# A macaron block on one core: V's second arrangement copied by VectorE ahead of its addition of the joined heads, not by two transfers

## What is computed

```
x = x + 0.5 * ffn(layernorm(x))
x = x + mla(layernorm(x))
x = x + 0.5 * ffn(layernorm(x))
```

```
h = shift_token(x)
q, k, v = split(h @ wqkv)                    # 8 heads of 64
q = l2norm(q) * qs;  k = l2norm(k) * ksc
q, k = rotary_xpos(q, k)
o = local_attention(q, k, v)                 # windows of 64 tokens, each looks at itself and the one before
x = x + o @ wo
h = layernorm(shift_token(x)) * lg + lb
a, g = split(h @ w1 + b1)
x = x + (a * gelu(g)) @ w2 + b2
```

## Time and profile before

| | before |
|---|---|
| median of 3 runs | 2024.47 us (2022.63 to 2025.84) |
| profiled execution | 2021.37 us, its span 2019.6 us |
| TensorE matmul busy | 84% |
| VectorE busy | 66% |
| ScalarE busy | 45% |
| GpSimd busy | 40% |
| the four engines in the turn from 257 to 303 us: TensorE, VectorE, ScalarE, GpSimd | 39.3, 35.1, 22.3, 24.2 us of 46.0 |

### The profile page before, as it was taken

How to read it: one execution, slowest core, us unless ns; L and a number is a source line. 1 busy time by engine, 2 the same in 40 slices (tenths; PEclk the granted TensorE clock), 3 DMA queues, 4 the chain that set the end, 5 groups by cost and what they waited for, 6 DMA issues and landing times. The chain is left out here.

```text
span 2019.6 us, 47886 instructions
## 1 busy us (share of the span) xinstructions
PE 1697.2 (84%) x19752; PEld 990.3 (49%) x19818; DVE 1336.6 (66%) x2021; ACT 916.4 (45%) x1455; POOL 799.7 (40%) x561
## 2 busy tenths in 40 slices
PE   3678888888889887799999994778888998988886
PEld 2345555555455554455555552445555555555543
DVE  4567776677766664577777764567777666667752
ACT  2234444454455443155555552344544554445442
POOL 3445445555554451100000002455555544555530
PEclk9789999999999999789999997889999999999998
DMA  4344454544444452322222200444344445554441
GB/s 144 40 77 67 75 76 75 86 72 69 75 73 75 77 78 54 98 74 83 80 75 92 92 22 7 67 73 86 69 67 73 77 68 82 77 92 80 76 84 32
DMA packets 82762, 148.55 MB, mean 74 GB/s; under 512 B 15039, under 2 KB 25715, under 8 KB 80371
## 3 DMA queue, kind: packets, MB, share of 16 engines
q1 hardware_dynamic: 81771, 142.81, 38.0%
q10 hardware_dynamic: 776, 2.68, 0.3%
HBM read 66.00 MB, written 16.52 MB: 41 GB/s over the span
## 5 line engine op out<-in xcount | busy, mean ns | idle before, releaser
L958 POOL TENSOR_TENSOR QK<-QK,RB 128x1024 f32<-128x1024 f32 x128 | 302.9, 2367 | 441.6 <-DMA RB<-RN 441.0
L798 DVE SCALAR_TENSOR_TENSOR TP<-banks,cols,tab 128x1024 f32<-128x1024 f32 x256 | 321.1, 1276 | 113.4 <-PE banks L462 88.8
L952 POOL TENSOR_TENSOR QK<-TP 128x512 f32<-128x512 f32 x128 | 164.8, 1287 | 252.1 <-DVE TP L798 193.6
L1295 ACT ACTIVATE PTL<-banks 128x1024 f32<-128x1024 f32 (+1 forms) x192 | 168.5, 885 | 168.5 <-PE banks L1202 168.5
L1370 DVE TENSOR_REDUCE NM<-banks 128x2 f32<-128x1024 f32 (+3 forms) x256 | 203.4, 821 | 57.2 <-PE banks L1171 56.1
L654 ACT ACTIVATE SQ<-banks 128x512 f32<-128x512 f32 x128 | 76.6, 599 | 290.0 <-PE banks L462 290.0
L821 DVE TRANSPOSE_TENSOR_REDUCE MX<-banks 128x16 f32<-128x512 f32 x256 | 160.3, 683 | 55.0 <-PE banks L499 55.0
L839 DVE TENSOR_TENSOR OT<-banks,OT 128x512 f32<-128x512 f32 x128 | 85.4, 688 | 151.8 <-DMA OT<-sums_d 138.3
L462 PE MATMUL banks<-HTH,wqkv_h 128*128 128x512 f32 x256 | 124.8, 487 | 68.4 <-POOL HTL L944 41.9
L953 POOL TENSOR_TENSOR QK<-TP 128x512 f32<-128x512 f32 x128 | 165.4, 1292 | 0.0
L532 PEld LDWEIGHTS banks<-PT,V 128*64 128x64 f32 x4096 | 128.5, 138 | 72.9 <-issue 47.5
(11 more groups left out here) (181 smaller groups left out, 3372.6 us busy)
## 6 DMA issues: line engine op xcount, KB each, us to landing
RB<-RN SPq DMA_DIRECT2D x512, 64.0 KB, 4.0
OT<-sums_d SPq DMA_DIRECT2D x128, 256.0 KB, 4.0
V<-V SPq DMA_DIRECT2D x32, 512.0 KB, 6.0
V<-V SPq DMA_DIRECT2D x32, 384.0 KB, 7.1
RB<-vars_d SPq DMA_DIRECT2D x32, 256.0 KB, 3.3
rows_d<-HIGH SPq DMA_DIRECT2D x32, 256.0 KB, 3.0
QS<-rows_d SPq DMA_DIRECT2D x32, 256.0 KB, 2.8
KS<-rows_d SPq DMA_DIRECT2D x32, 256.0 KB, 3.1
```

The source lines that it names most:

```text
L798: nc.vector.scalar_tensor_tensor(out=TP[:, o:o + 2, :], in0=BK[4 + z][:, :].unsqueeze(1).to_broadcast([P, 2, T]), scalar=q, in1=tab[:, e, ...
L952: nc.gpsimd.tensor_tensor(QK[:, m, 0, :], TP[:, 2, :], TP[:, 1, :], ALU.subtract)
L958: nc.gpsimd.tensor_tensor(QK[:, m, :, :], QK[:, m, :, :], RB[:, m, :].unsqueeze(1).to_broadcast([P, 2, T]), ALU.mult).then_inc(S["nr_ok"], 1)
L1295: nc.scalar.activation(PTL[:, G % 2, h0:h0 + 2, f * T:f * T + WIDTH_T[f]], PAIR[at_t(m) % RING][:, :, 0:WIDTH_T[f]], ACT.Exp).then_inc(S[" ...
```

## The change

The two transfers that fill V1 go, with SP's task `values`. VectorE gets a task `copy_values(u)` with the same two copies as `tensor_copy`: 64 partitions x 2048 and 64 partitions x 1536 elements of fp32. It waits for ScalarE's fourth slice of the unit (ve_ok) and, from the second unit on, for the attention that read the V1 of the unit before (pv_in). It stands in VectorE's list behind `statistics` and ahead of `residual`. The semaphore v1_ok now counts 1 a unit and not 32, and `attend` waits accordingly.

```
-                        def values(u):
-                            sp.wait_ge(S["ve_ok"], 4 * (u + 1))
-                            sp.dma_start(V1[0:W, :, :], V0[0:W, :, :]).then_inc(S["v1_ok"], 16)
-                            sp.dma_start(V1[W:P, 1:NT, :], V0[W:P, 0:NT - 1, :]).then_inc(S["v1_ok"], 16)
-
...
-                            run(values, n - 1)
...
-                            pe.wait_ge(S["v1_ok"], 32 * (u + 1))
+                            pe.wait_ge(S["v1_ok"], u + 1)
...
+                        def copy_values(u):
+                            dve.wait_ge(S["ve_ok"], 4 * (u + 1))
+                            if u >= 1:
+                                dve.wait_ge(S["pv_in"], 4 * u)
+                            nc.vector.tensor_copy(V1[0:W, :, :], V0[0:W, :, :])
+                            nc.vector.tensor_copy(V1[W:P, 1:NT, :], V0[W:P, 0:NT - 1, :]).then_inc(S["v1_ok"], 1)
+
...
                             run(statistics, n + 2)
+                            run(copy_values, n)
                             run(residual, n - 1, 7)
```

## The result

The changed kernel takes 2076.21 us (median of 4 runs, 2074.74 to 2077.93) against 2024.82 us before. Its ratio is 1.0245, 95% interval 1.0202 to 1.0288. The prediction on record was 2077.6 us. Its profiled execution took 2076.58 us, its span 2074.8 us.

A forecast was written before the change was run, and what follows sets the result against it. A chain through several engines, with GpSimd's L958, L944, L958 ahead of the scores, bounds each turn. 18 x 1.79 + 10 x 2.09 = 53.1 us on 2021.4 gives 2074.5, carried to the median 2077.6 us; range 2030 to 2104.

The forecast's parts named there:

- The chain: Feed-forward turn of about 45 us: a microsecond lost on GpSimd between 257.6 and 263.5 is lost for the whole turn.
- The removal at nothing: V1's two transfers per turn land some 17 us before `attend` reads them, so removing them is worth zero.
- The copies' duration: The two VectorE copies ahead of `residual` take 1.18 and 0.91 us, together 2.09 us.
- The one COPY in the earlier trace: SBUF to SBUF fp32 COPY of 512 elements, 365 ns, taken as half the PSUM slope to estimate the copies.
- the full-slope end: Upper estimate of the copies at the PSUM slope of 1.07 ns an element: 2.33 and 1.79, together 4.12 us.
- Hidden by VectorE's own queue at either slope: The copies fit VectorE's gap before `rotate` at 262.93; even 4.12 us end at 261.5 and `residual` at 262.9.
- The port: Copies block GpSimd's L958, L944, L958 on SBUF: +1.79 us in 18 turns, +2.09 in 10, 53.1 us; chance 0.59.
- Its sign: In the trace after, the second L958 starts about 5.7 us behind the last V slice instead of 3.9.
- rows 8: Trace rows of L318 beside L952/L953 and L969 beside L832, read as VectorE and GpSimd each waiting for the other's whole instruction.
- Half absorbed: Rival: VectorE's 1.27 us idle ahead of the maxima takes part of each 1.9 us; 18 us, 2042 us, chance 0.12.
- GpSimd keeps the port: Rival: VectorE gets in only behind GpSimd's third queued instruction, `rotate` 4.1 us late; 79 us, 2103 us, chance 0.09.
- hidden after all: Rival: a one-source copy doesn't stop GpSimd, so the copies fit VectorE's gap; 2024.5 us, chance 0.12.

The follow-up runs named there:

- the doubled L944: The kernel before, with GpSimd's low part of the tokens (L944) computed twice, one after the other, and no VectorE copy: 2079.7 us, ratio 1.0267.
- the two norms on VectorE: The kernel before, multiplications of blocks 0 and 1 by RB moved from GpSimd to VectorE: 2019.2 us; also with GpSimd's rotation ahead of block 2's multiplication: 2008.4 us.
- the reductions: The changed kernel with each of the two VectorE copies written as a tensor_reduce, maximum over one element: 2026.0 us, ratio 1.001.

## Why the prediction was right

- **The chain** (RB, first L958, L944, second L958, scores) is what sets the turn: shown by the doubled L944 in one direction (+1.36 us for +1.18) and less fully by the two norms on VectorE in the other (-0.35 and -0.52 us for -0.9): downward it has a neighbour about half a microsecond away, which the prediction didn't look for.
- **The removal at nothing**: right, 2026.7 us alone.
- **The copies' duration**: 1.18 and 0.91 us said, 1.21 and 0.96 measured where nothing disturbs them. The one COPY in the earlier trace rows was the right neighbour, and the full-slope end (2.33 and 1.79) is close to what the reductions take, 2.28 and 1.75.
- **Hidden by VectorE's own queue at either slope**: right, by the reductions.
- **The port**: right in kind and counted right (18 turns VectorE first, 10 GpSimd first). A little oversized: 1.79 and 2.09 us a turn, 53.1 in all, against 1.44 and 1.57 us at the end of the second L958 (7.63 and 7.26 us behind the fourth slice, 6.19 and 5.69 before), and 44.2 us added to GpSimd's times. Its sign was too strong in the same way: the second L958 starts 4.87 us behind the last slice in the mean, and not 5.7 (3.62 before, and not 3.9). A copy and a GpSimd instruction overlap somewhat at their edges: the first L958 above ended 2.22 us behind the copy, where alone it takes 2.35.
- **What was read from rows 8**: that they show both directions for two-input instructions. They show one, GpSimd's L969 lengthened beside VectorE's L832. The VectorE instructions that wait there, L318, have one SBUF source. The sum doesn't use the other direction.
- **What was missing**: the clock, to which the prediction gave nothing: 9 to 19 us by the two comparisons above, with the reserve made there. The oversized term and the missing one nearly cancel, so that 2077.6 against 2076.2 is luck: the reasoning was good to some 10 us, not to 1.4.
- "Half absorbed" was wrong since L944 slips as well, by 1.26 us in the mean; "GpSimd keeps the port" was wrong since VectorE got in behind each one instruction, as L318 had in the earlier trace rows; "hidden after all" was wrong since a one-source copy in this mode does stop GpSimd.

## What to carry to other kernels

Before work goes to VectorE's idle time, look at what GpSimd does in that window: a fast SBUF copy takes GpSimd's time too, and if GpSimd is on the chain there, the cheap copy is the costly one. A reduction over one element, a ScalarE copy, or the same copy a few microseconds earlier was free here. A transfer that lands 17 us ahead of its reader is already free: without it this kernel took 2026.7 us, as before, so replacing it had nothing to gain.

## What the runs showed of the hardware

- An fp32 SBUF copy of 64x2048 on VectorE takes 1.22 us and makes a GpSimd SBUF instruction beside it longer by most of that (3.18 us and not 2.35); a reduction that moves the same elements takes 2.28 us and leaves GpSimd at 2.37 us. Both read one SBUF source.
- Where both queues were full, the two engines took turns, one instruction each in the turns shown. A 4-element VectorE instruction of 0.17 us was recorded at 2.33 us.
- TensorE idle for 2.36 to 2.54 us ahead of the projection went with a granted clock of 1.2 GHz over at least the next 3.4 us in 12 of 28 turns, and in none once the idle time was filled; four turns with 2.53 to 3.05 us idle kept 2.4 GHz.
- VectorE multiplies 128x1024 from two SBUF tensors in 1.23 us undisturbed, GpSimd in 2.37.
